# Value half of the last layer's context projections moved into the first cross attention, and a later copy of turned items in the rotated projections

## The reference, cut to what matters

```python
x = x + _L0_xattn_ref(_layernorm(x), ctx, ...)      # 16 heads of 32, queries from x, keys and values from ctx, int8-quantised wq and wp
...
def _L1_xattn_ref(draft_hidden, context_hidden, Wq, Wk, Wv, Wo, ...):
    q = _rms_norm((draft_hidden @ Wq.T).reshape(bsz, draft_len, H, HD), q_norm_w)
    kv_in = jnp.concatenate([context_hidden, draft_hidden], axis=1)
    k = _rms_norm((kv_in @ Wk.T).reshape(bsz, total_len, KVH, HD), k_norm_w)
    v = (kv_in @ Wv.T).reshape(bsz, total_len, KVH, HD)
    q = _rope(q, draft_position_ids);  k = _rope(k, full_position_ids)
    ...
```

## Time and profile of the kernel before

| what | us |
|---|---|
| median of three executions | 2729.94 |
| the profiled execution, its own time | 2728.3 |
| span from its first to its last instruction | 2726.6 |
| PE busy | 2479.4 (91% of the span) |
| DVE, ACT, POOL busy | 1704.5, 1154.6, 934.5 |
| mean granted TensorE clock | 0.951 of full speed |
| the first cross attention | 351 to 578 |
| routing and context projections | 959 to 1139 |
| rotated projections of the last layer | 1694 to 1838 |

### The profile page before, as it was taken

One profiled execution on the slowest core, in us unless ns is written; L12 is line 12 of the kernel. 1 busy time (PEld: TensorE's weight loads), 2 busy tenths in 40 slices (PEclk: granted clock), 3 DMA queues, 4 the chain that ended last, 5 costly groups with the idle time before them and its releaser, 6 DMA issues. The chain is left out here.

```text
span 2726.6 us, 48715 instructions
## 1 busy us (share of the span) xinstructions
PE 2479.4 (91%) x14967; PEld 2033.7 (75%) x14968; DVE 1704.5 (63%) x3211; ACT 1154.6 (42%) x2389; POOL 934.5 (34%) x943
## 2 busy tenths in 40 slices
PE   7999788879899999799997998997999998999998
PEld 7888666658688887588875886665777787888887
DVE  4536847769777666676675566866555535666564
ACT  2103256623343334455553233757655522444443
POOL 4203201134333234423333212753333312355554
PEclk9999989989899989899998988998999989999999
DMA  5544122125622055477774432444222131666664
GB/s 191 154 140 114 28 93 77 46 91 168 179 68 65 15 166 182 147 220 223 195 223 105 131 68 96 151 125 126 73 70 72 55 129 63 182 163 159 147 163 73
DMA packets 304547, 336.59 MB, mean 123 GB/s; under 512 B 149231, under 2 KB 220063, under 8 KB 302578
## 3 DMA queue, kind: packets, MB, share of 16 engines
q1 hardware_dynamic: 233170, 256.24, 30.1%
q0 software_dynamic: 20640, 51.74, 9.7%
q10 hardware_dynamic: 50560, 26.34, 3.3%
HBM read 235.70 MB, written 98.56 MB: 123 GB/s over the span
## 5 line engine op out<-in xcount | busy, mean ns | idle before, releaser
L898 PE MATMUL e_psum<-e_up_hi,hT_hi 128*128 x672 | 244.9, 365 | 14.5 <-DVE hT_lo L867 11.0
L900 PE MATMUL e_psum<-e_up_hi,hT_lo 128*128 x672 | 237.0, 353 | 0.0
L899 PE MATMUL e_psum<-e_up_lo,hT_hi 128*128 x672 | 236.4, 352 | 0.0
L1938 POOL TENSOR_TENSOR joint_a_p<-joint_a_p,joint_a_rinv 112x487 f32<-112x487 f32 x128 | 125.5, 1002 | 187.5 <-DVE joint_a_rinv L1992 187.1
L1569 POOL TENSOR_TENSOR self_a_p<-self_a_p,self_a_mx 112x448 f32<-112x448 f32 x96 | 96.1, 1002 | 205.8 <-DVE self_a_mx L1626 205.8
L898 PEld LDWEIGHTS e_psum<-e_up_hi,hT_hi 128*128 128x128 f32 x672 | 127.6, 190 | 34.7 <-issue 24.5
L794 ACT ACTIVATE e_gate<-e_psum 128x352 f32<-128x352 f32 (+1 forms) x86 | 44.5, 517 | 247.0 <-PE e_psum L900 246.6
L1997 DVE TENSOR_REDUCE joint_a_mx<-joint_psum 112x1 f32<-112x487 f32 x128 | 84.9, 663 | 101.4 <-PE joint_psum L1963 100.7
L873 DVE TENSOR_TENSOR hT_lo<-e_psum,hT_hi 128x256 fp32r<-128x256 f32 (+2 forms) x138 | 55.7, 435 | 144.8 <-ACT hT_hi L812 144.8
L1660 ACT ACTIVATE self_a_p<-self_a_p 112x448 f32<-112x448 f32 x128 | 71.6, 574 | 168.1 <-POOL self_a_p L1569 114.9
L1211 POOL TENSOR_TENSOR p_p_z<-p_p_straight,p_p_crossed 128x512 f32<-128x512 f32 x70 | 98.4, 1407 | 112.5 <-DVE p_p_crossed L1193 110.5
(11 more groups left out here) (574 smaller groups left out, 7483.0 us busy)
## 6 DMA issues: line engine op xcount, KB each, us to landing
e_up_raw<-in_L_ffn_w SPq DMA_DIRECT2D x64, 512.0 KB, 5.0
e_up_raw<-in_L_ffn_w SPq DMA_DIRECT2D x64, 352.0 KB, 4.1
e_dn_raw<-in_L_ffn_w SPq DMA_DIRECT2D x16, 1024.0 KB, 5.5
q_all<-p_p_t_stage ACTq DMA_DIRECT2D x56, 256.0 KB, 2.3
e_dn_raw<-in_L_ffn_w SPq DMA_DIRECT2D x16, 512.0 KB, 6.3
x_first<-q_all SPq DMA_DIRECT2D x32, 224.0 KB, 2.7
v_ctx<-front_c_v_stage SPq DMA_DIRECT2D x24, 250.0 KB
x_others<-k_ctx SPq DMA_DIRECT2D x8, 750.0 KB, 5.3
```

What stands on the lines that cost most here:

```text
L898: pe.matmul(out, lhs[0], rhs[0], start=k == 0, stop=False)
L899: pe.matmul(out, lhs[0], rhs[1], start=False, stop=False)
L900: return pe.matmul(out, lhs[1], rhs[0], start=False, stop=k == n_k - 1)
L1938: pool.tensor_tensor(p[:, r, 0:S], p[:, r, 0:S], rinv[:, r:r + 1].to_broadcast([T, S]), ALU.mult).then_inc(p_ready, 1)
```

## The change

The values leave `ContextRopePart`, which then has one product for each item, four banks for them, and no second weight. A new `ContextValuesPart` `v` does the 24 value items inside the first cross attention, in three steps for each item: six matmuls; six matmuls, with the split of the next item's context slice (125 tokens, one raw buffer); copy by DVE, load of the item after next, and store. Its weight is loaded and split first (`fv`). It writes to bank 7, which OutNormPart uses too: nine items run before OutNormPart first needs the bank, the others take the two gaps of each sequence, between `added` and the turn of the normed rows, and between `ht_ready` and the next sequence's turn. The values go to a buffer of their own in memory (`v_ctx4`). `beside_context_values` writes the order. Besides, `RopeQkvPart`'s ACT generator issues the copy and store of the turned item at the end of its step, behind the square and the scaling.

```diff
@@ RopeQkvPart, scalar
                     act.activation(w_hi[:, u, ks, :], w_raw[:, u, ks, :], ACT.Copy).then_inc(hi_ready, 1)
-                i = step - LR
-                if 0 <= i < n_rot:
-                    n, t = i // TT, i % TT
-                    act.wait_ge(z_used, i + 1)
...
                     last.then_inc(z_ready, 1)
+                i = step - LR
+                if 0 <= i < n_rot:
+                    n, t = i // TT, i % TT
+                    act.wait_ge(z_used, i + 1)
+                    reuse(act, t_stored[i % 3], 16 * (i // 3))
+                    src = ps[:, T_BANKS[i % len(T_BANKS)], :].rearrange("p (c t) -> p c t", c=4)
+                    act.activation(t_stage[:, i % 3, :, :], src, ACT.Copy).then_inc(t_ready, 1)
+                    act.wait_ge(t_ready, i + 1)
+                    to = q_to[n * D:(n + 1) * D] if n < 4 else k_to
+                    act.dma_start(to[:, t * 128:(t + 1) * 128].rearrange("(c p) t -> p c t", p=128),
+                                  t_stage[:, i % 3, :, :]).then_inc(t_stored[i % 3], 16)
                 yield
@@ CrossAttentionPart
-        N_S, N_T, O_RING = len(s_banks), len(t_banks), 4
+        N_S, N_T, O_RING = len(s_banks), len(t_banks), 2
@@ OutNormPart, tensor: before the turn of the normed rows, and before the turn of the quantised output
+                        if others_in_bank:
+                            others_in_bank(pe, 2 * b + 1)
...
+                        if others_in_bank:
+                            others_in_bank(pe, 2 * b)
@@ ContextRopePart
-                for m in values_at(i):
-                    n, u = m % CCH, m // CCH % 2
-                    if m == 0:
-                        pe.wait_ge(w_ready, 2 * KC)
-                    reuse(pe, v_ready, m - len(v_banks) + 1)
-                    products(pe, ps[0:CT, v_banks[m % len(v_banks)], :], lambda k: (c_hi[:, u, k, tok(n)], c_lo[:, u, k, tok(n)]),
-                             lambda k: (w_hi[:, 1, k, :], w_lo[:, 1, k, :]), KC).then_inc(v_mm, 1)
...
+class ContextValuesPart:
...
+        def sync(sp):
+            def load(i):
+                b, n = i // CCH, i % CCH
+                reuse(sp, c_ready, i)
+                sp.dma_start(c_raw[:, :, 0:CT], core.ins["ctxT"][b][:, :, n * CT:(n + 1) * CT]).then_inc(c_in, 16)
+            sp.wait_ge(padded, 1)
+            load(0)
+            yield
+            load(1)
+            yield
+            for i in range(n_items):
+                yield
+                yield
+                if i + 2 < n_items:
+                    load(i + 2)
+                sp.wait_ge(v_ready, i + 1)
+                sp.dma_start(v_to[i // CCH, i % CCH, 0:CT, :], v_stage[:, i % 2, :]).then_inc(v_stored[i % 2], 16)
+                yield
...
+        def scalar(act):
+            def split_high(i):
+                act.wait_ge(c_in, 16 * (i + 1))
+                reuse(act, v_mm, i - 1)
+                act.activation(c_hi[:, i % 2, :, :], c_raw[:, :, :], ACT.Copy).then_inc(c_hi_ready, 1)
...
+        def tensor(pe):
+            yield
+            yield
+            for i in range(n_items):
+                u, out = i % 2, ps[0:CT, bank, :]
+                if i == 0:
+                    pe.wait_ge(w_ready, KC)
+                pe.wait_ge(c_ready, i + 1)
+                reuse(pe, v_ready, i)
+                bank_free(pe, i)
+                for k in range(KC):
+                    pe.matmul(out, c_hi[:, u, k, 0:CT], w_hi[:, k, :], start=(k == 0), stop=False)
+                    pe.matmul(out, c_hi[:, u, k, 0:CT], w_lo[:, k, :], start=False, stop=False)
+                    last = pe.matmul(out, c_lo[:, u, k, 0:CT], w_hi[:, k, :], start=False, stop=(k == KC - 1))
+                    if k == KC // 2 - 1:
+                        yield
+                last.then_inc(v_mm, 1)
+                yield
+                yield
...
+def beside_context_values(order, at_start):
+    done_a, done_o, placed, at = -2, -1, [], {}
+    half = 4
+    for n in range(at_start):
+        first, second, third = (half, half, half + 1) if n < 2 * at_start - 14 else (half, half + 1, half + 2)
+        for h in (first, second, third):
+            at.setdefault(("a", h), []).append("v")
+        half = third
+    for b in range(B):
+        for start in (8 * b + 4,) + (8 * b + 8,) * (b + 1 < B):
+            at.setdefault(("o", start), []).append("v")
+            at.setdefault(("o", start + 1), []).append("v")
+            at.setdefault(("a", start + 18) if start + 18 <= order.count("a") - 2 else ("o", start + 1), []).append("v")
...
+        if here in (("a", 0), ("a", 1), ("a", 2)):
+            placed += ["fv", "fv"]
+        if here in (("a", 2), ("a", 3)):
+            placed += ["v"]
...
@@ decoder, cross1
+                    at_start = 9
...
+                    fv = FirstWeightPart(g, "fv", ins["L1_xattn_Wv"], wq, wv_lo)
+                    f = FirstWeightPart(g, "f", ins["L0_ffn_wq"][0], first_hi, first_lo, behind=fv)
+
+                    def bank_free(pe, i):
+                        n = i - at_start
+                        if n >= 0:
+                            pe.wait_ge(o.ht_ready if n % 2 else o.added, n // 2 + 1)
...
                     LandedPart(g, "landed", last_queries)
-                    g.run(["landed"] + order[:90] + ["f"] + order[90:130] + [n for name in order[130:138] for n in (name, "f")] + order[138:])
+                    g.run(["landed", "fv"] + beside_context_values(attention_order(a, o, 8, 8, gap=0.95), at_start))
@@ decoder, r2c4
-                    c = ContextRopePart(g, "c", "L1_xattn_Wk", "L1_xattn_Wv", k_ctx, v_ctx, ctx_tabs, 1e-6, (0, 1, 2), (3, 4), (5, 6), last_context)
+                    c = ContextRopePart(g, "c", "L1_xattn_Wk", k_ctx, ctx_tabs, 1e-6, (0, 1, 2, 3), (5, 6), last_context)
```

More of the change, by code:

```diff
@@ L2106, in __init__ @@
         rows_out = g.sems(f"{name}_rows_out", 2)
-        self.ht_ready, attention.o_used = ht_ready, (lo_ready if turned_in else oq_ready if quantise_in else t_done)
+        self.added, self.ht_ready, attention.o_used = added, ht_ready, (lo_ready if turned_in else oq_ready if quantise_in else t_done)
         o_split = hi_ready if quantise_in else lo_ready
@@ L2507, in __init__ @@
         expo = g.sb(f"{name}_expo", [CT, heads])
[L2508 to L2512, removed]
+        t_stage, = last_stores.tiles
+        tabs_in, k_stored = (g.sems(f"{name}_{n}", 2) for n in ("tabs_in", "k_stored"))
+        (raw_in, c_in, padded, w_hi_ready, w_ready, c_hi_ready, c_ready, k_mm, square_done, x_read, ss_done, ms_ready, expo_set, z_added,
+         rstd_done, z_ready, z_used, t_ready) = (
+            g.sem(f"{name}_{n}") for n in ("raw_in", "c_in", "padded", "w_hi_ready", "w_ready", "c_hi_ready", "c_ready", "k_mm", "square_done",
                                            "x_read", "ss_done", "ms_ready", "expo_set", "z_added", "rstd_done", "z_ready", "z_used",
-                                           "t_ready", "v_ready"))
-        last_stores.leave(g, k_stored + v_stored, 8 * n_items)
+                                           "t_ready"))
+        last_stores.leave(g, k_stored, 8 * n_items)
         self.steps = 1 + n_items + LR
[L2518 to L2526, removed]
         def tok(n):
@@ L2584, in split_context @@
                 reuse(act, k_mm, (b - 1) * CCH)
-                reuse(act, v_mm, (b - 1) * CCH)
                 act.activation(c_hi[:, b % 2, :, :], c_raw[:, :, :], ACT.Copy).then_inc(c_hi_ready, 1)
-            def split_weight(n):
-                act.wait_ge(raw_in[n], 16)
-                for k in range(KC):
-                    act.activation(w_hi[:, n, k, :], w_raw[:, n, k, :], ACT.Copy).then_inc(w_hi_ready, 1)
-            split_weight(0)
+            act.wait_ge(raw_in, 16)
+            for k in range(KC):
+                act.activation(w_hi[:, k, :], w_raw[:, k, :], ACT.Copy).then_inc(w_hi_ready, 1)
             split_context(0)
-            split_weight(1)
             yield
@@ L2872, with __init__ @@
 class FirstWeightPart:
-    def __init__(self, g, name, src, hi, lo):
+    def __init__(self, g, name, src, hi, lo, behind=None):
         core = g.core
-        raw = g.sb(f"{name}_raw", [128, 2, D])
+        self.raw = raw = behind.raw if behind else g.sb(f"{name}_raw", [128, 2, D])
         w_in, hi_ready, self.ready = g.sems(f"{name}_in", 2), g.sem(f"{name}_hi_ready"), g.sem(f"{name}_ready")
@@ L2881, in sync @@
         def sync(sp):
+            if behind:
+                sp.wait_ge(behind.ready, KC)
             for c in range(KC):
@@ L3451, in attention_order @@
     return order + extra + ["o"] * (n_o - done_o)
+def beside_context_values(order, at_start):
[11 more added lines that the diff above has]
+            at.setdefault(("a", start + 18) if start + 18 <= order.count("a") - 2 else ("o", start + 1), []).append("v")
+    for name in order:
+        placed.append(name)
+        if name == "a":
+            done_a += 1
+            here = ("a", done_a)
+        else:
```

(10 more changed lines are left out.)

111 lines of the change are left out of this document (72 added, 39 removed).

## The result

| | before | after |
|---|---|---|
| median of four runs each | 2730.61 us | 2754.68 us (2750.22 to 2757.68) |
| span of the profiled execution | 2726.6 us | 2748.5 us |
| ratio, 95% interval | | 1.0088 [1.0073, 1.0104] |

The change makes the kernel 0.9% slower. The forecast was 2755.

The account below looks back on a forecast made before the run. PE, busy for 91% of the span, was taken as the common limit, with stages differing. First cross attention +59, routing -26 and rotated projections -8 gave +25 us on 2728.3, about 2755; range 2716 to 2775.

Parts of the forecast that it names:

- Start, +30: First cross attention, up to the ninth score step: weight loads and nine early value items delay it by 30 us.
- Steady state, +26: First cross attention, ninth to last score step: a sequence takes 28.45 us instead of 23.38, adding 26 us.
- Tail, +3 (0 to 8): End of the first cross attention: the last two value items in bank 7 add 3 us, between 0 and 8.
- Routing, -26 (-38 to -18): Routing and context projections: PE loses 67 us, but the key chain then binds, so 26 us less, bounds -38 to -18.
- Rotated projections, -8 (0 to -10): Last layer's rotated projections: with the copy last, PE's idle in 33 steps goes, 8 us less, between 0 and -10.
- (a): First cross attention: the gaps take the chunks, the stage grows some 29 us, kernel faster at 2715; chance 0.18.
- (b): Whole kernel: first cross attention's growth of 30 to 40 us cancels against the two gains, 2730; chance 0.1.
- (c): First cross attention's start: late value slices hold ACT, +15 to +28 us, kernel at 2770 to 2783; chance 0.1.
- (d): Rotated projections: the copy's new place does nothing as another wait holds the turn, +8 us, 2763; no separate chance.

Follow-up runs that it names:

- with one product: Changed kernel with 2 of the 12 matmuls of each value item, all loads, splits, copies and stores kept; first eight score steps 73.0 us against 75.2.
- with one slice: Changed kernel with only the first value slice loaded, all later items splitting that same slice again; first eight score steps 73.2 us, first cross attention 293.1.
- the first experiment: Kernel before, with only ACT's copy and store of the turned item moved last in the rotated projections; 2715.49 us against 2728.96, ratio 0.9952.

## Why the prediction was right, and where its steps were off

**The verdict and the sum.** +25 was forecast and +22 profiled, +24 in the medians. It was right because it walked through the order instead of dividing work by room. Some luck is in it: the first stage cost 8 us more than forecast (293.4 us long, where 280 to 290 had been named), the two gains came out 10 us larger, and these errors cancel.

**Start, +30.** Measured +31.6. First exponential 362.9 forecast, 363.0 measured; exponentials of the fourth step 391.4 and 393.2; ninth step 425.4 and 426.7. The reasons held too (weight in two loads in series, two chunks of 1.40 us in a step with 1 us of room). Their sizes held less well: a load of the weight took 3.4 us from issue to split, not 4.5, and ACT waited 0.94 us more for the last slice, so two errors of about 1 us cancel. And the runs with one product and with one slice show that two limits lie on top of each other here, which the prediction did not say.

**Steady state, +26.** Measured +27.7. The steps were forecast at 7.6, 6.8, 7.95 and 6.1 and are 7.8, 6.7, 8.2 and 6.1. The wait for `hT_lo` is there. The lower clock took 2.9 us (167.5 less 6 x 28.8 - 8.2 = 164.6), and 3 had been put for it.

**Tail, +3 (0 to 8).** This term was mis-sized: +7.7 in the profile, and +9 to +10.5 in four other runs with this tail. The prediction counted only the value items in bank 7, at full clock: each of the last two took about 4.5 us for its products instead of 2.80, as the granted clock was 0.81 from 612 us to the stage's end. And it did not follow the other thing that the new order moved there: `f`, whose raw tile is now shared with `fv`, splits its slices in the tail. Its last two loads are issued at 628.05, when VectorE has split its first slice, and that split stands in VectorE's order behind the copy of a value item at 626.73. In the run with `f` moved out of the tail, 4.4 us are left (47.4 against 43.0).

**Routing, -26 (-38 to -18).** Measured -30.0. The chain is the one named, with 14.5 us for three items forecast (its terms as listed make 14.6) and 14.4 to 15.2 measured, and moving copy and store out of it shortened it to 12.7. Items 4 to 23 took 94.3 us (96), which is 27.1 less than before; the items ahead of them gave 3.3 us (2), and what follows the last square took 0.4 us more (1). The lower clock did come, 0.82 granted against 0.93; what it cost by itself no run shows.

**Rotated projections, -8 (0 to -10).** Measured -14.1, outside the bounds. The step that failed is "PE's 0.2 to 0.3 us of idle in each of 33 steps". The record gives a product 0.39 us, but products start every 0.23. In the earlier trace rows the turn begins 3.69 us after the one before; twelve products and a turn need 3.20. The recorded idle of 0.29 us began only when the last product's modelled end had passed: from that product's start to the turn were 0.67 us before and are 0.23 now, 0.44 in all. Over all steps the interval fell from 3.63 to 3.20, so the right term was 33 times 0.43. The last product ahead of the first turn of the earlier trace rows, at 1756.84:

```profile
1756.17 0.39 PE L142 MATMUL p_psum<-p_p_w_hi,hT_lo 128*128 128x512 f32 x1
```

**The rivals.** (a) had the gaps take the chunks: a full sequence at 25 to 26 us. Its premise on the clock came true, 0.94 against 0.86 granted in the first stage, and the sequences still took 28.8, with a wait of 1.69 us for bank 7's `hT_lo` ahead of a chunk. Even with most of the products gone they took 25.4 at full clock. (b) did not occur, (c) is refuted above, (d) by the first experiment.

## What to carry to other kernels

Idle time beside a loop is not room: follow each moved piece to the wait ahead of which it stands, and ask what that wait would have hidden. Price a pipelined engine by start to start of the same instruction in two steps, not by the idle time that a record shows. A copy or store that nobody waits for yet belongs behind the work that somebody waits for; here ScalarE gave 14 us for it in one stage and 7 in another.

## What had not been expected of the hardware

A small operation of VectorE beside a large one of GpSimd ended only with it. In the routing stage the 125x4 multiply-add L2629, 0.77 us by itself, took 2.81 us from 1122.51 and ended at 1125.32, just after GpSimd's split of 3.37 us ended at 1125.30 (rows above). So it is with all seven splits that it meets in this trace and all seven in the kernel before: it ends 0.02 to 0.04 us behind the split, after up to 2.95 us. In the tail the quantising step L2248 took 1.38 us beside GpSimd's 1.36 us split, and 0.43 us else; in the run with one slice that split had ended before it, and it took 0.43 there too. What the two engines share is not shown.

A load that is issued right behind another transfer on SP's queue lands later: the queries' load of the first cross attention lands in 5.3 us as a median after the change, and did in 3.1 before, with the same bytes. Ahead of it stand now a slice's load and a store of finished values, issued within some 1.5 us. The slice's load is not the reason: in the run with one slice, with the store alone ahead, the median is still 5.0 us. No run took the store away. A value slice takes 3.4 us as a median. The Trainium skill (DMA: Bandwidth & Descriptors, Specifications) gives 512 bytes as the least transfer for the full rate; the slices have rows of 500, and their median is no longer than that of the value weight with rows of 2 KB (3.6 us), so this trace shows no penalty just below that size:

```profile
cross_v_c_raw<-in_ctxT SPq DMA_DIRECT2D x24, 250.0 KB, 3.4
...
x_others<-q_d SPq DMA_DIRECT2D x7, 224.0 KB, 5.3
...
cross_fv_raw<-in_L_xattn_Wv SPq DMA_DIRECT2D x4, 256.0 KB, 3.6
```

Two slots for the raw slices were not tried.
